# Attended rows of a decoder turned and divided by VectorE in 32x32 blocks, and one more wait for GpSimd in cross attention

## The reference, cut to what matters

```python
xn = layer_norm(x, ln1_w[i], ln1_b[i])               # four decoder layers
q, k, v = split(xn @ Wi.T + bi)                      # 16 heads of 16
attn = softmax(q @ k.T / 4 + mask)                   # causal, with ALiBi slopes
x = x + (attn @ v) @ Wo.T + bo                       # "attended rows" are attn @ v
xn = layer_norm(x, ln2_w[i], ln2_b[i])
x = x + gelu(xn @ W1.T + b1) @ W2.T + b2
...
x = _layernorm(x + cross_attention(x, ctx))          # no mask, ReLU FFN behind it
```

## Time and profile before

| | us |
|---|---|
| median of 3 runs | 3473.02 (3469.25 to 3474.62) |
| the profiled execution's own time | 3473.01 |
| its span in the trace | 3471.3 |
| TensorE busy in the span | 3252.6 (94%) |
| VectorE busy in the span | 2675.1 (77%) |
| ScalarE busy | 2299.8 (66%) |
| GpSimd busy | 1648.4 (47%) |

### The profile page before, as it was taken

One profiled execution on the slowest core, in us unless ns is written; L12 is line 12 of the kernel. 1 busy time (PEld: TensorE's weight loads), 2 busy tenths in 40 slices (PEclk: granted clock), 3 DMA queues, 4 the chain that ended last, 5 costly groups with the idle time before them and its releaser, 6 DMA issues. The chain is left out here.

```text
span 3471.3 us, 76257 instructions
## 1 busy us (share of the span) xinstructions
PE 3252.6 (94%) x29568; PEld 2158.1 (62%) x29568; DVE 2675.1 (77%) x5237; ACT 2299.8 (66%) x3540; POOL 1648.4 (47%) x1612
## 2 busy tenths in 40 slices
PE   5899999999999999999986887899999999999998
PEld 2566665666656666566653554566666666666665
DVE  4777777777777777777677888898888888888877
ACT  3677776777777777777745665566666666666665
POOL 2354453544535445353444433564444444544475
PEclk8999999999999999999997999899999999999999
DMA  3110111101111011110011212100000000000001
GB/s 117 37 38 29 41 52 34 38 29 41 49 37 38 29 41 49 37 38 29 29 45 59 65 55 69 59 13 27 27 1 27 1 27 1 27 1 27 1 13 37
DMA packets 104485, 122.87 MB, mean 35 GB/s; under 512 B 20320, under 2 KB 92256, under 8 KB 101984
## 3 DMA queue, kind: packets, MB, share of 16 engines
q1 hardware_dynamic: 104128, 118.00, 10.4%
HBM read 49.35 MB, written 8.39 MB: 17 GB/s over the span
## 5 line engine op out<-in xcount | busy, mean ns | idle before, releaser
L2830 POOL TENSOR_TENSOR e_hT<-e_h,e_hT 128x512 f16<-128x512 f32 x512 | 613.5, 1200 | 605.7 <-ACT e_hT L2579 581.9
L1335 POOL TENSOR_SCALAR_AFFINE_SELECT PR<-PR 128x512 f32<-128x512 f32 (+1 forms) x384 | 307.4, 805 | 833.9 <-ACT PR L1002 832.1
L2573 ACT ACTIVATE e_h<-e_h,e_b 128x512 f32<-128x512 f32 x512 | 365.4, 714 | 416.3 <-DVE e_h L2659 416.3
L1214 DVE TENSOR_REDUCE mx<-maxima_pair 128x4 f16<-128x1024 f32 (+1 forms) x384 | 469.2, 1222 | 213.5 <-PE maxima_pair L694 213.4
L93 PE MATMUL bank<-xT,w_half 128*128 128x512 f16 x2400 | 568.5, 387 | 5.7 <-DVE xT L1157 4.2
L1002 ACT ACTIVATE PR<-scores_pair 128x1024 f32<-128x1024 f32 x384 | 391.6, 1020 | 102.4 <-PE scores_pair L706 101.9
L93 PEld LDWEIGHTS bank<-xT,w_half 128*128 128x128 f16 x2400 | 227.6, 99 | 272.6 <-issue 31.3
L2517 PE MATMUL bank<-VS,e_hT 128*128 128x256 f16 x3072 | 389.1, 273 | 6.2 <-DVE VS L2622 4.6
L2517 PE MATMUL bank<-e_w,e_hT 128*128 128x256 f16 x3072 | 388.7, 273 | 4.3 <-POOL e_hT L2830 4.1
L93 PE MATMUL bank<-w_half,hT 128*128 128x256 f16 x3072 | 364.3, 276 | 8.0 <-ACT oT L957 5.8
L2517 PEld LDWEIGHTS bank<-VS,e_hT 128*128 128x128 f16 x3072 | 300.2, 98 | 113.1 <-DVE VS L2622 5.1
(11 more groups left out here) (215 smaller groups left out, 6352.2 us busy)
## 6 DMA issues: line engine op xcount, KB each, us to landing
QS<-QK SPq DMA_DIRECT2D x240, 128.0 KB, 2.1
KS<-QK SPq DMA_DIRECT2D x192, 128.0 KB, 2.1
PR<-in_expert_weights SPq DMA_DIRECT2D x16, 1024.0 KB, 5.1
stage<-in_weights SPq DMA_DIRECT2D x48, 256.0 KB, 3.4
xT<-in_x SPq DMA_DIRECT2D x8, 512.0 KB, 3.8
xT_f<-xT SPq DMA_DIRECT2D x8, 512.0 KB, 3.7
stage<-xT_f SPq DMA_DIRECT2D x4, 1024.0 KB, 5.2
out<-stage SPq DMA_DIRECT2D x8, 512.0 KB, 3.7
```

Source lines behind the costliest of these rows:

```text
L1214: dve.tensor_reduce(out, src, AX.X, ALU.max, negate=True).then_inc(mx_in.sem, 1)
L1335: pool.affine_select(blocks, blocks, [[0, x], [1, P]], base=0, channel_multiplier=-1, compare_op=ALU.is_ge, fill=nothing).then_inc(past.se ...
L2573: act.activation(h32[r % 2][:, j, :], h32[r % 2][:, j, :], ACT.Gelu, bias=b1[:, e, m:m + 1], scale=1.0 / WS)\
L2830: pool.tensor_tensor(hT[r % 2][1][:, f, part], h32[r % 2][:, j, :], hT[r % 2][0][:, f, part], ALU.subtract)\
```

## The change

In the decoder TensorE's OS and OT turns, their PSUM banks and their semaphores go. VectorE does the work instead, quarter by quarter. `divide(n, c)` turns `OTs[:, c, :]` in 32x32 blocks (a `STREAM_TRANSPOSE`) into a new tile `turned`: each block of 32 columns then holds 16 values and the denominator of one head. It takes the reciprocals and multiplies the 16 values into one half of the blocks of `divided` (the old `On`), so that two quarters fill the blocks. `join_outputs(n, k)` turns a full `divided[:, k, :]` back into `OTs[:, 2k, :]`, from where `outputs_high` and `outputs_low` now read (SBUF, no longer PSUM). The features then stand in another order, and the output projection's weight rows and the value biases are permuted to match. `divide` of quarters 0, 1 and 2 is done in the body that attends to them, quarter 3 in the next body. In cross attention GpSimd's `add_bias` also waits until the roots have ended.

```diff
-            bank = tile(kind, "OS", t)[:, :].rearrange("p (h d) -> p h d", h=H)
-            dve.reciprocal(rden[:, t, :], bank[:, :, HD]).then_inc(rd_in.sem, 1)
-            dve.tensor_tensor(On[:, t, :].rearrange("p (h d) -> p h d", h=H), bank[:, :, 0:HD],
-                              rden[:, t, :].unsqueeze(2).to_broadcast([P, H, HD]), ALU.mult)\
+        def divide(n, c):
+            dve.wait_ge(o_in.sem, o_in.after(n, c + 1))
+            dve.wait_ge(on_in.sem, on_in.after(n, c))
+            dve.transpose(turned[:, :], OTs[:, c, :]).then_inc(turned_in.sem, 1)
+            blocks = turned[:, :].rearrange("p (b r) -> p b r", r=SQ)
+            dve.wait_ge(turned_in.sem, turned_in.after(n, c + 1))
+            dve.reciprocal(rden[:, c, :], blocks[:, :, HD]).then_inc(rd_in.sem, 1)
+            dve.wait_ge(rd_in.sem, rd_in.after(n, c + 1))
+            dve.wait_ge(joined.sem, joined.after(n - 1, c // 2 + 1))
+            to = divided[:, c // 2, :].rearrange("p (b r) -> p b r", r=SQ)[:, :, c % 2 * HD:(c % 2 + 1) * HD]
+            dve.tensor_tensor(to, blocks[:, :, 0:HD], rden[:, c, :].unsqueeze(2).to_broadcast([P, BL, HD]), ALU.mult)\
                .then_inc(on_in.sem, 1)
+        def join_outputs(n, k):
+            dve.wait_ge(on_in.sem, on_in.after(n, 2 * k + 2))
+            dve.transpose(OTs[:, 2 * k, :], divided[:, k, :]).then_inc(joined.sem, 1)
...
             if back:                       # VectorE, behind maxima (2,0)
-                outputs(kind, n, 0)
...
+                divide(n - 1, 3)
+                join_outputs(n - 1, 1)
...
                 norm2_scaled(n, group(g, -1))
+            if front:
+                divide(n, 0)
...
                 shrunk(kind, n, group(g, -2), 3)
+            if front:
+                divide(n, 1)
+                join_outputs(n, 0)
...
                     norm1(n + 2, group(g, 2))
+            if front:
+                divide(n, 2)
...
             if has(n - 1):                 # GpSimd in cross attention
                 query_key_low(n - 1, 0)
                 query_key_low(n - 1, 1)
+            if has(n - 1) and n + 1 < NG + start.LAG:
+                pool.wait_ge(start.rooted.sem, start.rooted.after(n + 1))
+            if has(n - 1):
                 add_bias(n - 1)
```

## The result

The changed kernel takes 3552.57 us (median of 4 runs, 3549.86 to 3555.66) against 3472.9 (3469.25 to 3474.62): 79.7 us more, a ratio of 1.0234 with a 95% interval of 1.0221 to 1.0246. The direction was forecast; the loss was forecast at 33 us, so its size was missed by more than a factor of two. The time lies just inside the outer bounds (3442 to 3555) and beyond the forecast's own range (3497 to 3540). The profiled execution has a span of 3552.1 us.

The account below looks back on a forecast made before the run. TensorE and VectorE were both taken as full at a body's start. 3473 + 21 (decoder bodies) + 15 (clock) - 3 (cross attention) = 3506 us; own range 3497 to 3540, outer bounds 3442 to 3555.

Parts of the forecast that it names:

- step 5: VectorE's new multiplications contending with GpSimd for SBUF: bounds nothing or .83 at each of four places, taken as +.08 a body.
- the share of bodies in which the clock falls: Waits at a body's start lower TensorE's clock in every second body, 1.00 us each: +15 us, bounds 0 and 52.
- the multiplication of a plain body by 31: Decoder: the sum of +.67 us a body, taken for all 31 steps between bodies: +21 us.
- What bounds, and the removed work: Decoder: TensorE and VectorE full at a body's start; 3.56 us of TensorE's turns go, most of it becoming waiting.
- The price of a turn: VectorE's 512-column turn takes .69 us; a division 1.31, a division with a joining turn 2.00.
- Steps 1 to 4: Decoder, us a body: body's start +.28, last OT turn -.52, T2 +.67, row scores (1,1) +.16.
- The OT turn: TensorE's last OT turn, behind the row scores (2,2) at a body's start, goes: -.52 us a body.
- Steps 1 to 5: Decoder: the four changes of path and the contention sum to +.67 us a body, +21 us over 31 bodies.
- the new wait before T2: T2 waits for `shrunk` 1 behind quarter 0's division: +.67 us a body, said to take up that much of a clock fall.
- Cross attention: GpSimd's held `add_bias` frees the root steps but meets the scalings: -.4 us a group, -3 us, bounds -25 to +19.
- B: Rival: VectorE's new work is dearer, by a port or a turn of .95: 2.23 us a body, 3554 us; chance .08.

Follow-up runs that it names:

- filled kernel: The changed kernel with the second values product worked two times more, where TensorE waited at a body's start: 3518.47 us, ratio 1.013.

## Why the prediction was right in direction and wrong in size

Three terms of the sum failed: the contention of step 5, the share of bodies in which the clock falls, and the multiplication of a plain body by 31, which left out what the bodies that load weights lose. The rest came out near its forecast.

**What bounds, and the removed work.** Right. TensorE had no gap and lost 2.6 of its 52.21 busy microseconds a body (49.59 at a full clock), and nothing of it was gained, since at the body's start VectorE was as full, and ScalarE's exponentials were waited for next.

**The price of a turn.** Right: .70 where .69 was taken. The estimate from the page "VectorE: DVE Perf Modes" of the Trainium skill (section "The three transpose paths") was .71, and the trace agrees. A division is 1.37 and not 1.31, with the joining turn 2.11 and not 2.00: the .04 between dependent operations add up.

**Steps 1 to 4.** The places were right, the sizes short. These are TensorE's key scores (0,0) and its first `shrunk` matmuls in the kernel before:

```profile
1180.32 0.39 PE L706 MATMUL scores_pair<-QS,KS 64*128 64x256 f16 x4
```

```profile
1136.78 2.78 PE L93 MATMUL bank<-w_half,hT 128*128 128x256 f16 x24
```

From the key scores (0,0) to the row scores (2,2) it is now 1186.34 - 1178.06 = 8.28 us, before 1188.17 - 1180.32 = 7.85: +.43 for a forecast .28, of which .17 is the longer divisions. The OT turn gave its .52. From `shrunk` to T2 it is now 1208.66 - 1186.88 = 21.78, before 1157.72 - 1136.78 = 20.94: +.84 for a forecast .67, since the division is longer by .06 and T2 starts .15 behind the end of `shrunk` 1 (1208.10 + .42 = 1208.52), where a hand-over of .06 was taken. From T2 to the row scores (1,1) it is 12.22 for 12.02, +.20 for .16. In sum a body with a full clock and without contention is .43 - .52 + .84 + .20 = .95 longer, as 53.40 is against 52.45, where .59 was summed.

**Step 5, contention, failed.** "One hit in ten bodies or so at each" of two places, .08, was taken from the even low half of the earlier trace rows, beside which GpSimd was idle (its next selection starts at 1183.48, the low half ends at 1182.81). At quarter 0 no multiplication was hit; at quarter 1 27 of 32 were, most at .94 - .43 = .51, because GpSimd's selection starts as its row additions end, at the same moment in most bodies. That is the .49 by which 53.89 stands above 53.40. The page "SBUF — State Buffer" of the Trainium skill (section "Who interferes with whom") has the rule, and the trace agrees with its .94; whether an operation is hit depends on what GpSimd does at that place, and so is read from its row there, not from a row elsewhere.

**The bodies that load weights** were not priced: the forecast is a plain body's sum times 31. In the filled kernel, where no plain body's clock falls, the 28 bodies are 1566.27 - 1516.73 = 49.5 us longer than before, 28.0 in the 19 plain ones (1.5 each) and 21.5 in the nine that load (2.4 each, six of these with a lower clock). What those lose more was not set apart by a run. Steps 1 to 5 were forecast at 21.

**The clock failed in how many bodies fall.** The length of the waits was right (2.80 forecast, 3.06 found, 1.00 of it ScalarE's). But "one of two rows fell, so I take every second body": 22 of 28 bodies had a lower clock, 13 of the 19 plain ones and all nine that load. Two rows for a share were too few. The trace before holds a third wait of 3.07 at that place, and there the clock fell too:

```profile
1296.38 0.61 PE L690 MATMUL maxima_pair<-KS,QS 63*128 63x128 f16 x8 [3.07 <-DVE mx L1214]
```

```profile
1296.00:1300.00 4.00, 3.62 (x25) 2.67 (x26) 2.32 (x4) 1.81 (x3) 1.09 (x1) 0.50 0.00 0
```

And "of which the new wait before T2 takes up its .67" names the wrong wait. In the body of 55.03 us, which had the fall, these are the row scores (2,2), T2 and the row scores (1,1):

```profile
1240.71 0.39 PE L695 MATMUL maxima_pair<-KS,QS 63*128 63x128 f16 x8
...
1263.19 0.63 PE L654 MATMUL bank<-ident,z 128*128 128x128 f32 x4 [0.66 <-DVE x L1177]
...
1275.91 0.39 PE L695 MATMUL maxima_pair<-KS,QS 63*128 63x256 f16 x4 [0.60 <-DVE mx L1208]
```

T2 still waits .66. The chain of VectorE's that it waits for is itself let go by maxima, so by TensorE's row scores; when TensorE is late, that chain is as late. The row scores (2,2) wait no more, where they waited .54: the maxima (2,1) were let go ahead of the slow matmuls. So a fall costs 55.03 - 53.90 = 1.13 there, against the full-clock body with the same contention, and 16.1 / 13 = 1.24 on average against the same plain bodies of the filled kernel. The forecast 1.00 was near it by luck. Filling the waits gave back 27.6 us in the 28 bodies and 3552.6 - 3518.5 = 34 in all, where 15 were forecast.

**Cross attention.** Right: -3 forecast, -2.3 between the two profiles, no measurable difference alone; most of what the root steps gain the scalings lose. On this the page "SBUF — State Buffer" says that the order of issue decides who is blocked; `add_bias` took 2.34 to 2.37 in both kernels, so VectorE was the one that waited each time, and no run turned the order round.

In the 28 bodies the sum is 49.5 + 27.6 = 77 us, where 21 + 15 - 3 = 33 was forecast for the program. Of the rivals, B (VectorE's new work is dearer, by the port) was half of the truth: its price came at one place, not four, and its 3554 is near the result only because the clock and the bodies that load made up the rest. What no argument saw is that the order on VectorE, and not the amount of work moved there, made the loss: the prediction listed VectorE's idle time of .55 as slack, and did not ask what the same work costs behind the next maxima.

## What to carry to other kernels

When work moves from a full engine to one with a quarter of its time free, look at where in the period that time lies: the same 7.0 us of VectorE a body (2 x 1.37 + 2 x 2.11) cost 80 us in one order and gained 43 in another. Work taken from TensorE in front of a wait that ends last does not shorten anything; it turns into waiting, and here waits of 1.00 and 1.52 us close together went with a lower clock behind them, so a cover that goes has to be priced with both. A sum over bodies is made for each kind of body: nine of 28 lost 33 of the 77 us. A delay is taken up by a later wait only if what is waited for does not itself follow the delayed engine.

## What the runs showed that was not expected

- Useless matmuls pay: 24 of them a body, on an engine that is the bound, took 34 us off, since they stand in waits of 1.00 and 1.52 us and hold the granted clock of every plain body at 1.00.
- The waits at the start of a body, 1.00 and 1.52 us one behind the other, went with a lower clock in 13 of 19 plain bodies; 1.69 us at the start and 1.26 elsewhere went with none in any of them.
- A multiplication of VectorE and a selection of GpSimd that meet cost up to .51 us of the one in 24 bodies, and about .2 of the other in five.
- The stretch from the decoder's last body but one to the end, most of it code that did not change but for GpSimd's wait, differs by up to 16 us between profiles (1786.3 to 1802.5), so differences of 5 us between two versions of the decoder are read from its bodies, not from the sum.
